# Two transfers of an attention kernel issued at other places in ScalarE's sequence

## The reference, cut to what matters

```python
h = tok(x)                                   # 64 x 196 x 192
h = h + attn(layernorm(h), ...)              # first layer, 12 heads of 16
xx = layernorm(h)                            # the residual of the second layer's block
x1 = xx + attn2(ln(xx, ln1_g, ln1_b), ...)   # second layer
h = h + (x1 + mlp(x1) + moe(...))
```

```python
atten = softmax(q @ k.T * SCALE)
out = (atten @ v) @ w_proj.T + b_proj
```

## Time and profile before

| | us |
|---|---|
| median of 3 runs | 3173.27 |
| lowest, highest | 3169.94, 3174.86 |
| the profiled execution's own time | 3171.36 |
| its span, first to last instruction | 3169.6 |

### The profile page before, as it was taken

One profiled execution on the slowest core, in us unless ns is written; L12 is line 12 of the kernel. 1 busy time (PEld: TensorE's weight loads), 2 busy tenths in 40 slices (PEclk: granted clock), 3 DMA queues, 4 the chain that ended last, 5 costly groups with the idle time before them and its releaser, 6 DMA issues. The chain is left out here.

```text
span 3169.6 us, 95506 instructions
## 1 busy us (share of the span) xinstructions
PE 2756.1 (87%) x31491; PEld 2128.4 (67%) x31491; DVE 2320.9 (73%) x5326; ACT 1878.0 (59%) x3798; POOL 1671.7 (53%) x1957
## 2 busy tenths in 40 slices
PE   4999379998999988989998858988984999999998
PEld 3888345555555555555555538888874888888887
DVE  4888477887878787878787726766655777777776
ACT  3888256676666666666666637666642444444443
POOL 2777325455554666666666441556554444444444
PEclk8999688999999999999999969999986999999999
DMA  5564245667666666677767635444433444444443
GB/s 140 162 188 125 58 111 136 157 151 161 147 153 151 157 165 160 159 170 163 162 162 164 152 81 139 135 128 132 129 107 95 67 67 67 68 67 67 67 67 50
DMA packets 515433, 395.07 MB, mean 125 GB/s; under 512 B 223136, under 2 KB 488386, under 8 KB 515138
## 3 DMA queue, kind: packets, MB, share of 16 engines
q1 hardware_dynamic: 431426, 310.47, 40.2%
q0 software_dynamic: 38496, 46.38, 8.3%
q10 hardware_dynamic: 45216, 34.34, 4.6%
HBM read 232.59 MB, written 155.42 MB: 122 GB/s over the span
## 5 line engine op out<-in xcount | busy, mean ns | idle before, releaser
L701 DVE TENSOR_REDUCE a_mx<-a_mxp 98x4 f32<-98x784 f32 x768 | 747.5, 973 | 278.5 <-PE a_mxp L850 275.3
L540 ACT ACTIVATE a_pt<-a_st 98x784 f32<-98x784 f32 x768 | 633.9, 825 | 364.9 <-PE a_st L836 363.8
L1609 POOL DMA_INDIRECT out_dram<-f_yo,f_idg x202 | 329.8, 1633 | 417.2 <-DVE f_yo L1950 380.7
L481 POOL TENSOR_TENSOR a_cf<-a_ctxs,a_rec 128x1176 f32<-128x1176 f32 x64 | 171.5, 2680 | 456.1 <-DMA a_rec<-a_recip 456.1
L1687 ACT ACTIVATE f_hf<-f_bank,f_b1c 128x256 f32<-128x256 f32 x606 | 253.9, 472 | 236.5 <-PE f_bank L924 236.3
L865 PE MATMUL a_pv<-a_pt,a_vp 98*32 98x196 f32 x6144 | 359.6, 353 | 5.4 <-issue 4.4
L836 PE MATMUL a_st<-a_qst,a_kst 49*128 49x196 f16 x3072 | 268.1, 254 | 78.8 <-DMA a_qst<-a_mrow 54.2
L2112 PE MATMUL f_bank<-f_w2h,f_hh 128*128 x1212 | 298.9, 247 | 14.4 <-DVE f_hl L1934 13.0
L2113 PE MATMUL f_bank<-f_w2h,f_hl 128*128 x1212 | 298.2, 246 | 0.0
L2114 PE MATMUL f_bank<-f_w2l,f_hh 128*128 x1212 | 298.2, 246 | 0.0
L850 PE MATMUL a_mxp<-a_kst,a_qst 48*128 48x196 f16 x3072 | 264.9, 251 | 27.5 <-DVE a_mx L701 22.7
(11 more groups left out here) (324 smaller groups left out, 8367.6 us busy)
## 6 DMA issues: line engine op xcount, KB each, us to landing
a_rec<-a_recip SPq DMA_DIRECT2D x256, 147.0 KB, 4.9
t_rows<-in_x_dram SPq DMA_DIRECT2D x84, 392.0 KB, 5.9
a_qst<-a_qk SPq DMA_DIRECT2D x256, 110.2 KB, 3.1
a_kst<-a_qk SPq DMA_DIRECT2D x256, 110.2 KB, 3.8
f_xg<-f_listed SPq DMA_DIRECT2D x101, 264.0 KB
a_qk<-a_qkh SPq DMA_DIRECT2D x128, 196.0 KB, 3.1
a_qk<-a_qkl SPq DMA_DIRECT2D x128, 98.0 KB, 3.4
a_qk<-a_qkh SPq DMA_DIRECT2D x128, 98.0 KB, 2.5
```

What stands on the lines that cost most here:

```text
L540: act.activation(pt[k % PT][:].rearrange("p j a t -> p j (a t)"), st_ps[0:half_t, :, 0:unit_t], ACT.Exp, scale=sm_scale).then_inc(exp_s, 1)
L701: dve.tensor_reduce(mx[:, a, :, 2 * p:2 * p + 2].rearrange("p q j -> p j q"), mx_ps[0:half_t, :, 0:unit_t].rearrange("p j (q t) -> p j q t ...
L1609: pool.indirect_dma_start(out, bass.IndirectOffsetOnAxis(ap=idg[i % 3][:, t:t + 1], axis=0), yo[i % 3][:, t, :], None, compute_op=ALU.add) ...
```

## The change

The store of the normalised rows moves from slot 0 to slot 4 of the step, second layer only. The load of the residual rows moves from slot 8 to slot 6, both layers. Both keep their waits, their sizes and their queue. In the text of the program the placing of the second image's maxima (slot 3) now stands ahead of the store's place, since the slots are written in their order; it stays in slot 3.

```diff
-                    if k == 0 and kinds.get("L") == 1:
+                    if k == 3 and "C" in kinds:
+                        place_maxima(s, par, 1)
+                    if k == 4 and kinds.get("L") == 1:
                         u = s + 3
                         wait(act, xx_s, 4 * (u - UL + 1))
                         act.dma_start(of_units(r_rows, u, 1), xx[:]).then_inc(res_s, 16)
-                    if k == 3 and "C" in kinds:
-                        place_maxima(s, par, 1)
-                    if k == 8 and "O" in kinds:
+                    if k == 6 and "O" in kinds:
                         u, b = s - 1, (par + 1) % 2
                         waits(act,
                               (xo_s, OUTS * (u - 1) + 1),
```

## The result

The changed kernel is slower. Its median is 3230.03 us over 4 runs (3223.95 to 3239.13), against 3174.07 us over 4 runs of the kernel before on the same chip: a ratio of 1.0178, 95% interval 1.0149 to 1.0207. The profiled execution took 3239.13 us (span 3237.4). The forecast was 3127 us, the range ended at 3168.

A forecast was written before the change was run, and what follows sets the result against it. Bound by TensorE's maxima-row wait, the a_rec loop through GpSimd and SP's queue, loaded by the DMA engines. 31 x 0.6 + 31 x 0.9 = 46.5 us off the profiled 3171.4 gave 3124.9, as median 3127; range 3100 to 3168.

The forecast's parts named there:

- three chains: TensorE's order with its maxima-row wait; the loop from projection through a_rec and GpSimd back; SP's issue queue up to a_sums.
- I put this at nothing: ScalarE's queue: the residual load's wait for the first output rows, done 0.5 us before ScalarE asks, costs nothing.
- both must shrink for the step to shrink: Attention step: maxima-row wait and a_rec's landing must both come earlier; the smaller gain counts.
- I take 0.6 a step: First layer: the residual load's move was forecast to save 0.6 us a step.
- 0.9 less: Second layer: both moves together were forecast to save 0.9 us a step, bounds 0 and 1.4.
- 0.31 a step: Second layer: the store's move by itself gains up to 0.31 us, the reciprocal's wait for a_sums.
- GpSimd's cover: GpSimd's 5.3 us a step of waiting for a_rec hides up to 1.2 us lost waiting for the moved store.
- chains A and B: TensorE's order with the maxima-row wait (A); projection, reciprocal, output rows, a_rec, GpSimd, next projection (B); both end together.
- upper bound of 1.0 a step: Residual load's move: most it could save, 1.0 us a step, if both the maxima-row and a_rec gains go whole.
- Partly handed on: Rival, chance 0.14: maxima wait goes, a_rec lands hardly earlier, the projection waits for a_cn; 12 us gained, 3161.
- Nothing moves: Rival, chance 0.11: same DMA work, contention goes to the store SP waits for, loss equals gain; 3173.
- Slower: Rival, chance 0.09: the load runs beside the last key store, delaying SP's queue; 9 us lost, 3182.

The follow-up runs named there:

- the fastest kernel: Changed kernel with the negation's factor moved from VectorE to ScalarE's copy and SP issuing a_sums ahead of output and input rows: 3055.71 us, ratio 0.9661.
- the filler: Changed kernel with 14 unused TensorE matmuls added in slot 2: 3143.38 us, ratio 0.9942; the same added to the kernel before: 3117.08 us, ratio 0.9995.
- the late negation: Kernel before with VectorE's slot 0 negation done in slot 1, no transfer moved: 3259.21 us, ratio 1.0327.
- the first two: Changed kernel with the negation taken off VectorE, its factor applied in ScalarE's existing copy: 3161.75 us, ratio 0.9977.
- the first and third: Changed kernel with SP issuing a_sums earlier in its queue, VectorE's negation left as it is: 3148.66 us, ratio 1.0117.

## Why the prediction was wrong

**What bounds the kernel.** The three chains were there and did what was said of them, but a fourth was missing: VectorE's maxima, through a negation that ends when GpSimd lets it. I read GpSimd's chain only for when it *ends* (1468.66) and not for what it shuts out while it *runs*. The row was in the trace: 0.73 us for an instruction that takes 0.17 alone, ending 0.04 us after `a_cf`. So was the other half: 14 falls of TensorE's clock in a kernel whose layers stand at 0.98 and 0.99, and steps with a fall over 2 us longer than the others.

**Part 1, the residual load.** The maxima row's wait went whole and `a_rec` came 1.0 us earlier, the top of the 0.6 to 1.0 forecast. "I put this at nothing" holds for ScalarE: in the step of 1468 us the load waits for the output rows, but TensorE waits 1.91 us for the same ones, so nothing else is held. The step that failed is the next one, from "both must shrink for the step to shrink" to "I take 0.6 a step": it took both chains' gains as the step's gain, and put at nothing, without a word, what the shift does on VectorE and to TensorE's clock. Both chains did shrink. But starting the step earlier moved the negation from the end of one product of GpSimd into the start of the next, from 0.70 to 1.34 us in the mean, and the steps with a fall went from 8 to 34 of 56. Measured was 0.23 us less a step in the first layer where the clock didn't fall, and 0.81 us more in the mean; in the second layer, for a forecast of 0.9 less, 0.86 more.

**Part 2, the store.** Forecast 0.31 a step, 9.6 us; alone it gave 0.42%, 13 us (4 to 23), so the term was right in size. The reciprocal's wait for `a_sums` is no longer in the second layer's list with it alone, as forecast. But SP's longest low-part store of that layer was still 1.77 us; only with both moves it was 0.71. GpSimd's cover was still 92.0 / 23 = 4.0 us a step.

**The sum.** 46.5 us of gain were forecast and 56 of loss came. What came next after chains A and B was named rightly, `a_sums`, but it shows only with the negation gone. There the gain of the load's move is larger than its upper bound of 1.0 a step: the middle steps of the two layers take 20.5 and 20.6 us in the mean with it, and 22.4 and 22.2 with the load left in slot 8, 1.9 and 1.6 less.

**The rivals.** *Partly handed on*: no, TensorE's wait for `a_cn` is down to 0.3 us in the second layer. *Nothing moves*, with the rule that all queues share the 16 engines: the rule holds, its outcome here doesn't, `a_rec` did land sooner. *Slower* had the sign, and its mechanism appeared, past the 1.4 us a step that I had set as the mark (1.84). But it wasn't the cause: without the negation the wait is the same (40.6 us over 24 steps) and the kernel 2.0% faster, and the fastest kernel has 51.2 us of it over 25 steps. Its price is still open, as nothing was tried against it.

**Left open.** Why taking the negation off the kernel before costs 0.46% isn't settled; its wait for the maxima row grew from 23.8 to 32.1 us over 24 steps, which goes with it but explains nothing. Nor is it known why its falls didn't become fewer, and what the falls of the kernel before outside the long negations come from. That the idle time brings the clock down is shown by the filler and by the late negation; why some steps with a long negation escape (7 of 38) wasn't found.

## What to carry to other kernels

Before an engine's chain is pulled forward, read what it runs beside, now and afterwards: a short VectorE instruction whose record is far longer than its shortest (here 2.16 for 0.17 us) and ends within a few hundredths of a us of a GpSimd one is held by it, and will be held by the next one if they shift. A stall of 1 us on TensorE is to be priced by what the granted clock does after it, not by its length; here a step with a fall was about 2 us longer. When a forecast gain doesn't come, free the next constraint before giving the edit up: three edits that give 1.0178 for the first, 0.9977 for the first two and 1.0117 for the first and third, give 0.9661 together.

## What was not expected of the hardware

A negation of 98x24 numbers as a `tensor_scalar` took 0.17 us or, behind a GpSimd instruction, up to 2.16 in the changed kernel and 2.35 in the one with the filler; a reduction over the same numbers took 0.17 to 0.18 in all 126 cases. After TensorE was busy 0.88 of 2.0 us in slots 1 and 2, its granted clock was at the lower level from 1484.6 to 1491.4 us, 6.8 us in which it was busy throughout. Fourteen useless matmuls a step made the changed kernel 2.3% faster and the kernel before neither faster nor slower.
